# Transposes of the attention weights behind the first row of scores, and layer norm statistics taken one stage earlier

## The chip, the cores and the metric

One core of a Trainium2 chip runs one program. The metric is the device time of that program in microseconds, the median of several runs. The engines are TensorE (PE; its weight loads are listed as PEld), VectorE (DVE), ScalarE (ACT), GpSimd (POOL) and SyncE (SP), which here issues DMAs. Each runs its own list of instructions in order; semaphores connect them.

## The reference

The input x has 1024 tokens of 512 numbers (32 sequences of 32). Six layers follow one another, each added to x and each reading the layer norm of x:

```python
x = x + L0_xattn(layernorm(x), ctx)   # cross-attention, causal
x = x + L0_attn(layernorm(x))         # windowed, gated
x = x + L0_ffn(layernorm(x))          # 64 experts, top 8
x = x + L1_xattn(layernorm(x), ctx)   # cross-attention, 257 context rows, 16 heads of 64
x = x + L1_attn(layernorm(x))         # rotary attention, 16 heads of 32, alibi
x = x + L1_ffn(layernorm(x))          # 8 experts, top 2
# layernorm: (x - mean) / sqrt(var + 1e-5) over the 512 numbers of a token
```

The change touches the fourth and the fifth. In the fourth, each sequence of 32 tokens attends to the 257 rows of its own context: scores, softmax over the 257, weights times context. All is in f32.

## The kernel before

x lies in SBUF throughout, as 8 tiles of 128 tokens (4 sequences each). Each stage has one function per engine (`cross_pe`, `cross_dve`, `cross_act`; `attention_pe`, ...), written out in the order in which the engine is to work; the order is by hand, with no planner. Counters (`Counts`) turn that order into semaphore values.

Fourth layer, `cross_pe`. The key projection is folded into the queries, so that for one sequence the scores are 4 rows of blocks (`rt`, 128 head-and-token rows each) by 257 context rows: `scores(b)` (L567), four matmuls in the program for each row of blocks, two instructions each. DVE takes the maxima of the four (`maxima`, L1091 to L1096), ACT the exponentials (L1321), DVE normalises (`normalise`, L1103, L1107) and signals `s_p`. `turn_weights` (L571) then transposes the weights on PE in three groups of four 128x128 blocks (all by L259): first the last context column, broadcast; then context rows 0 to 127; then 128 to 255. The groups alternate between two PSUM banks (TP), so a group waits until ACT has copied out the group two before it (`act_take`, L1223). `mix(b)` (L588) multiplies context by the turned weights in four steps over two other banks (PROJ), which DVE takes (`take_mix`, L1112). A tile on PE (L620) goes: for sequences 0 to 2, `turn_weights`, `scores(b + 1)`, `mix(b)`; for sequence 3, `turn_weights`, then `pe_turn_xn` (transposes of the next tile's normalised x, L271), then its `mix`; then the next tile's queries (L534, L555), heads (L601), `scores(0)` of the next tile between the two halves of the heads, and the output projection (L615). The last tile (`final`) has no next tile to prepare.

A tile on DVE (L1128) ends with `layernorm` of tile i + 2 (L709: statistics L713, aggregation L715, inverse root L692 to L706 in small steps on one column, normalise step L720), then `add_to_x(i)` (L1124, L1126). For i = 6 the layer norm is that of tile 0 for the fifth layer. After the eight tiles L1170 signals `s_end["xattn1"]`. SP waits for it to load the fifth layer's value weights, output weights (L1446) and the last layer's eight experts (L1577), in that order. Query and key weights are loaded earlier.

Fifth layer, `attention_pe`/`attention_dve` with `rope=True`. PE per tile: queries and keys (L302), `values` (L352), the value projection (L302), transposes of rotated queries and keys (L259), score matmuls of 32x32 (L329), transposes of the next xn (L259), output projection (L365). `scores` waits for ACT's copies of the turned queries and keys and, but for the first tile, for `take_out` (L855). DVE per tile: rotation of queries and keys (L757 to L761), `layernorm(i + 2)`, `take_out`, softmax (L818 to L841) with the additions to x (L801) in between. Ahead of the loop, with no `take_out`, stands `layernorm(dve, 1)`. The first value projection waits for its weights' load.

Of the kernel before, what the change touches and what calls it, by code (L numbers as in the profile page):

```python
# [10 lines left out]
ALU = mybir.AluOpType  # L11
# [4 lines left out]
B, S, D = 32, 32, 512  # L16
TILES = B * S // P
# [14 lines left out]
EPS = 1e-5  # L32
# [33 lines left out]
def wait(eng, sem, value):  # L66

    if not isinstance(value, int) or value > 0:
        eng.wait_ge(sem, value)
# [35 lines left out]
def build(nc, t):  # L105
    with ExitStack() as ctx:
        def sb(name, words, dt=F32):
            return ctx.enter_context(nc.sbuf_tensor(name, [P, words], dt))[:, :]

        def sem(name):  # L110
            return ctx.enter_context(nc.semaphore(name))

        def carve(buf, base, *sizes):

            for n in sizes:
                assert base + n <= buf.shape[1], (base, n)
                yield buf[:, base:base + n]
                base += n


        x = sb("x", TILES * D)
# [20 lines left out]
        xn, xnT = carve(work, 0, D, D)  # L142
# [29 lines left out]
        def some(n, at=[0]):  # L172
            at[0] += n
            assert at[0] <= 1240, at
            return small[:, at[0] - n:at[0]]

        stats, mv, var, half, root, step = some(6), some(2), some(1), some(1), some(1), some(1)
        negmax, total, inv, restp = some(H), some(H), some(H), some(H)
        blockmask, causal, rshare = some(S), some(S), some(TILES)
        keymask = some(TILES * S)  # L180
# [21 lines left out]
        s_xn = sem("xn_ready")  # L202
# [17 lines left out]
        s_ctxT = [sem("ctx_columns_even"), sem("ctx_columns_odd")]  # L220
# [21 lines left out]
        def pe_project(pe, c, emit, banks=2):  # L242

            wait(pe, s_proj_free, c.proj.value(banks - 1))
            emit(bank[PROJ + c.proj.n % banks]).then_inc(s_proj, 1)
            c.proj.add()
# [7 lines left out]
        def pe_transpose(pe, c, pieces):  # L254

            wait(pe, s_tp_free, c.tp.value(1))
            to = bank[TP + c.tp.n % 2]
            for j, src in enumerate(pieces):
                done = nc.tensor.transpose(to[:, j * P:(j + 1) * P], src, ident[:, :])  # L259
            done.then_inc(s_tp, 1)  # L260
            c.tp.add()

        def pe_turn_xn(pe, c, parts, banks=2):
            c.xn.add()
            wait(pe, s_xn, c.xn.value())
            n = KD // parts
            for part in range(parts):
                def emit(to):
                    for j in range(n):
                        at = (part * n + j) * P  # L270
                        done = nc.tensor.transpose(to[:, j * P:(j + 1) * P], xn[:, at:at + P], ident[:, :])  # L271
                    return done
                pe_project(pe, c, emit, banks)
# [250 lines left out]
        def cross_pe(pe, c):  # L524
# [14 lines left out]
            def turn_q():  # L539
                for half_ in range(2):  # L540
                    wait(pe, s_proj_free, c.proj.value(1 - half_))
                    pe_transpose(pe, c, [q1[:, (half_ * 4 + j) * P:(half_ * 4 + j + 1) * P] for j in range(4)])
# [16 lines left out]
                    c.proj.add()  # L559
                    c.tp.add()  # L560

            def scores(b):
                c.ctxT[b % 2].add(16)
                wait(pe, s_ctxT[b % 2], c.ctxT[b % 2].value())
                for rt in range(4):
                    for j in range(KD):
                        done = nc.tensor.matmul(bank[SCORE + rt][:, 0:NCTX], qpv[:, j, b, rt * P:(rt + 1) * P],  # L567
                                                ctxT[b % 2][:, j * NCTX:(j + 1) * NCTX], start=(j == 0), stop=(j == KD - 1))
                    done.then_inc(s_s, 1)

            def turn_weights():  # L571

                c.p.add(4)
                wait(pe, s_p, c.p.value())
                pe_transpose(pe, c, [p1[:, (rt + 1) * NCTX - 1:(rt + 1) * NCTX].broadcast_to([P, P]) for rt in range(4)])
                for kc in range(2):
                    pe_transpose(pe, c, [p1[:, rt * NCTX + kc * P:rt * NCTX + (kc + 1) * P] for rt in range(4)])

            def mix(b, turned):

# [38 lines left out]

            def tile(final):  # L620
                for b in range(SEQS - 1):
                    turn_weights()
                    turned = c.tp.value()
                    scores(b + 1)
                    mix(b, turned)
                turn_weights()
                turned = c.tp.value()
                if not final:
                    pe_turn_xn(pe, c, 1)
                mix(SEQS - 1, turned)  # L630
                mixed = c.proj.value()
                if not final:
                    project_q(KD)
                    turn_q()
                    queries_wk()
                wait(pe, s_proj_free, mixed)
                out_heads(0)
                if not final:
                    wait(pe, s_proj_free, c.proj.value(1))
                    wait(pe, s_tp_free, c.tp.value())  # L640
                    scores(0)
                out_heads(1)
                project_out()
# [46 lines left out]
        def inverse_roots(dve, var, half, root, step):  # L690

            nc.vector.tensor_single_scalar(half.bitcast(I32), var.bitcast(I32), 1, ALU.logical_shift_right)  # L692
            dve.drain()
            nc.vector.tensor_scalar(root.bitcast(I32), half.bitcast(I32), -1.0, float(0x5F3759DF), ALU.mult, ALU.add)
            for _ in range(3):
                dve.drain()
                if var.free_size() == 1:
                    nc.vector.scalar_tensor_tensor(step, root, var, root, ALU.mult, ALU.mult)
                else:
                    nc.vector.tensor_tensor(step, root, var, ALU.mult)  # L700
                    dve.drain()
                    nc.vector.tensor_tensor(step, step, root, ALU.mult)
                dve.drain()
                nc.vector.tensor_scalar(step, step, -0.5, 1.5, ALU.mult, ALU.add)
                dve.drain()
                nc.vector.tensor_tensor(root, root, step, ALU.mult)  # L706
            dve.drain()

        def layernorm(dve, i):  # L709

            xt = x[:, bass.ds(i * D, D)]
            dve.drain()
            nc.vector.bn_stats(stats, xt)  # L713
            dve.drain()
            nc.vector.bn_aggr(mv, stats)  # L715
            dve.drain()
            nc.vector.tensor_scalar(var, mv[:, 1:2], EPS, None, ALU.add)
            dve.drain()
            inverse_roots(dve, var, half, root, step)
            nc.vector.tensor_scalar(xn, xt, mv[:, 0:1], root, ALU.subtract, ALU.mult).then_inc(s_xn, 1)  # L720

        def statistics(dve):

# [22 lines left out]
        def attention_dve(dve, st, c):  # L746
# [120 lines left out]
            def tile(i, ln=True, rest=False, tails=SEQS):  # L867
                seqs = iter(range(tails if st.cross else 0))

                def sums():  # L870
                    for _ in range(tails // 4):
                        for b in seqs:
                            sum_tail(b, i + 1)
                            break
                first(sums)
                if ln:
                    if st.gated and (not isinstance(i, int) or i + 2 < TILES):
                        dve.drain()
                        correct(i + 2)
                    layernorm(dve, i + 2 if not isinstance(i, int) else (i + 2) % TILES)  # L880
                take_out()
                if rest:
                    take_rest()
                if "v" not in st.by_act:
                    take("v")
                if rest:
                    take_turned_rest()

                def between():
                    if rest:  # L890
                        take_rest_out()
                    add_to_x(i, 0)
                softmax(i + 1, between, lambda: add_to_x(i, 1))
# [9 lines left out]
            if st.cross:  # L903
                dve.wait_ge(s_w["bias_vo0"], 16 * 3)
            if st.rope:
                layernorm(dve, 1)
            if "v" not in st.by_act:
                take("v")
            if st.cross:
# [151 lines left out]
        def cross_dve(dve, c):  # L1061
# [60 lines left out]
            def add_to_x(i):  # L1122
                xt = x[:, bass.ds(i * D, D)]
                dve_take(dve, c, lambda src: nc.vector.tensor_tensor(xt, xt, src, ALU.add))  # L1124
                dve.drain()
                nc.vector.tensor_tensor(xt, xt, bo1, ALU.add)  # L1126

            def tile(i, final):  # L1128
                for b in range(SEQS - 1):
# [531 lines left out]
```

## Time and profile before

| | us |
|---|---|
| median of 3 runs | 2520.74 |
| lowest, highest | 2514.85, 2523.68 |
| profiled execution, device time | 2523.09 |
| profiled execution, span of its instructions | 2521.2 |
| fourth layer (second cross-attention) | about 1296 to 2066 |
| fifth layer (rotary attention) | about 2066 to 2240 |

PE is the busiest engine; DVE is busy 44% of the span, ACT 13%. In all rows the start is counted in microseconds from the start of the span, and "idle <-" gives the idle time of the engine just before the instruction and what ended it. The granted clock (PEclk) is 1.00 at 2.4 GHz and 0.50 at 1.2 GHz; a value between is the mean of a stretch that had both.

### The profile page before, as it was taken

The numbers are of one execution on the slowest core, as the hardware profiler recorded it, in microseconds if no ns is written. First come the engines' busy times: TensorE is split into PE (matmuls) and PEld (weight loads), VectorE is DVE, ScalarE is ACT, GpSimd is POOL, SyncE is SP. The second block draws the span as 40 slices with busy tenths as digits, with TensorE's granted clock in tenths as the row PEclk, the third lists the DMA queues.
The fourth block names the chain that finished last, engine by engine and source line by source line (L and its number), as shares of the span: only waits on it lengthen the run. The fifth ranks groups of instructions, "written<-read, shape, count | busy, mean of one in ns | idle before, by whom it ended". The sixth has DMA issues, their size and how long they took to land. (4 is left out here: it accounts for less than half of the span.)

```text
span 2521.2 us, 48836 instructions
## 1 busy us (share of the span) xinstructions
PE 2324.2 (92%) x19338; PEld 1695.1 (67%) x19338; DVE 1116.2 (44%) x3030; ACT 321.9 (13%) x753; POOL 213.5 (8%) x266
## 2 busy tenths in 40 slices
PE   6999899997369999999979999999999999979999
PEld 5887688986258888888856766766766755544444
DVE  3666332333644444444334444444444436634333
ACT  0000011110001111111112222222222211100000
POOL 0000000000014333333310000000000000000000
PEclk8999899999579999999989999999999999989999
DMA  6224500002429999999951111111111132000000
GB/s 251 67 67 167 151 32 0 0 0 77 163 89 333 326 329 336 331 324 333 334 152 59 34 42 58 33 45 55 33 47 53 34 134 96 0 2 9 8 8 8
DMA packets 64677, 291.18 MB, mean 115 GB/s; under 512 B 9079, under 2 KB 9591, under 8 KB 55264
## 3 DMA queue, kind: packets, MB, share of 16 engines
q1 hardware_dynamic: 46976, 247.50, 27.1%
q0 software_dynamic: 16480, 40.62, 6.3%
q10 hardware_dynamic: 1152, 2.10, 0.2%
q8 instruction: 49, 0.80, 0.1%
q14 instruction: 20, 0.16, 0.0%
HBM read 268.45 MB, written 23.13 MB: 116 GB/s over the span
## 5 line engine op out<-in xcount | busy, mean ns | idle before, releaser
L493 PEld LDWEIGHTS psum<-work,arena 128*128 128x128 f32 x3072 | 354.4, 193 | 31.7 <-issue 30.8
L493 PE MATMUL psum<-work,arena 128*128 128x128 f32 x3072 | 355.0, 276 | 1.4 <-ACT work L1282 1.4
L296 PEld LDWEIGHTS psum<-work,arena 128*128 128x128 f32 x2560 | 293.0, 194 | 8.7 <-issue 4.8
L296 PE MATMUL psum<-work,arena 128*128 128x128 f32 x2560 | 293.8, 277 | 3.0 <-ACT work L1223 1.7
L672 PE MATMUL psum<-arena,work 128*128 128x512 f32 x512 | 233.9, 620 | 0.0
L567 PE MATMUL psum<-work,arena 128*128 128x257 f32 x1024 | 229.6, 381 | 0.8 <-DVE arena L1084 0.8
L1223 ACT COPY work<-psum 128x512 f32<-128x512 f32 (+2 forms) x200 | 102.6, 540 | 985.9 <-PE psum L259 835.7
L588 PE MATMUL psum<-work 128*128 128x512 f32 x512 | 225.7, 594 | 2.9 <-ACT work L1223 2.2
L567 PEld LDWEIGHTS psum<-work,arena 128*128 128x128 f32 x1024 | 192.1, 190 | 29.4 <-issue 1.2
L302 PE MATMUL psum<-arena,work 128*128 128x512 f32 x448 | 199.7, 597 | 1.4 <-ACT work L1223 1.4
L672 PEld LDWEIGHTS psum<-arena,work 128*128 128x128 f32 x512 | 101.0, 199 | 126.5 <-issue 126.2
L501 PE MATMUL psum<-arena,work 128*128 128x512 f32 x384 | 182.0, 610 | 2.0 <-DVE work L1035 2.0
L588 PEld LDWEIGHTS psum<-work 128*128 128x128 f32 x512 | 96.5, 190 | 113.3 <-issue 98.5
L365 PE MATMUL psum<-arena,work 128*128 128x256 f32 x640 | 156.0, 405 | 3.7 <-DVE work L855 2.4
L302 PEld LDWEIGHTS psum<-arena,work 128*128 128x128 f32 x448 | 83.1, 190 | 95.8 <-issue 93.7
L365 PEld LDWEIGHTS psum<-arena,work 128*128 128x128 f32 x640 | 129.6, 206 | 23.5 <-DVE work L855 2.6
L1112 DVE SCALAR_TENSOR_TENSOR arena<-work,psum 128x512 f32<-128x512 f32 x128 | 95.5, 746 | 101.5 <-PE psum L588 101.5
L259 PE MATMUL psum<-ident,work 128*128 128x128 f32 x616 | 95.9, 287 | 37.1 <-DVE work L720 20.5
L1091 DVE TENSOR_REDUCE small<-psum 128x1 f32<-128x257 f32 x128 | 54.2, 424 | 171.5 <-PE psum L567 170.5
L259 PEld LDWEIGHTS psum<-ident,work 128*128 128x128 f32 x616 | 72.0, 144 | 77.5 <-issue 40.5
L501 PEld LDWEIGHTS psum<-arena,work 128*128 128x128 f32 x384 | 68.1, 190 | 64.6 <-issue 61.8
L1041 DVE TENSOR_SCALAR work<-psum,small 128x512 f32<-128x512 f32 x64 | 48.0, 751 | 130.4 <-PE psum L501 102.4
(174 smaller groups left out, 2217.6 us busy)
## 6 DMA issues: line engine op xcount, KB each, us to landing
arena<-in_experts SPq DMA_DIRECT2D x64, 2304.0 KB, 10.0
work<-in_ctxT SPq DMA_DIRECT2D x32, 514.0 KB, 4.3
work<-in_ctx SPq DMA_DIRECT2D x32, 512.0 KB, 3.8
work<-in_ctx_tail SPq DMA_DIRECT2D x32, 450.0 KB, 3.4
arena<-in_experts SPq DMA_DIRECT2D x8, 1024.0 KB, 18.3
arena<-in_qkv SPq DMA_DIRECT2D x1, 6144.0 KB, 19.2
arena<-in_o SPq DMA_DIRECT2D x2, 2048.0 KB, 18.7
arena<-in_q SPq DMA_DIRECT2D x1, 2048.0 KB, 8.9
```

Of the source, the lines that this page charges most:

```text
L259: done = nc.tensor.transpose(to[:, j * P:(j + 1) * P], src, ident[:, :])
L296: done = nc.tensor.matmul(to[:, n * P:(n + 1) * P], w[:, j, at:at + P], src[:, j * P:(j + 1) * P], start=(j == 0), stop=(j == KD - 1))
L302: done = nc.tensor.matmul(to, src[:, j * P:(j + 1) * P], w[:, j, half_ * BANK:(half_ + 1) * BANK], start=(j == 0), stop=(j == KD - 1))
L365: done = nc.tensor.matmul(to[:, 0:D // 2], oT[:, j * P:(j + 1) * P], w[:, j, half_ * D // 2:(half_ + 1) * D // 2], start=(j == 0), stop=(j ...
L493: done = nc.tensor.matmul(to[:, n * P:(n + 1) * P], w[:, at:at + P], xgT[e % 2][:, j * P:(j + 1) * P], start=(j == 0), stop=(j == KD - 1))
L501: done = nc.tensor.matmul(bank[5 + e % 2], hid[e % 2][:, j * P:(j + 1) * P], w[:, j * D:(j + 1) * D], start=(j == 0), stop=(j == INTER // ...
L567: done = nc.tensor.matmul(bank[SCORE + rt][:, 0:NCTX], qpv[:, j, b, rt * P:(rt + 1) * P], ctxT[b % 2][:, j * NCTX:(j + 1) * NCTX], start=( ...
L588: done = nc.tensor.matmul(to, ctxr[b % 2][:, at:at + P], pT1[:, kc * 4 * P:(kc + 1) * 4 * P], start=(kc == 0), stop=(kc == 1))
L672: done = nc.tensor.matmul(to[:, 0:n], xnT[:, j * P:(j + 1) * P], w[:, j * n:(j + 1) * n], start=(j == 0), stop=(j == KD - 1))
L1091: nc.vector.tensor_reduce(negmax[:, rt:rt + 1], bank[SCORE + rt][:, 0:NCTX], AX.X, ALU.max, negate=True)
L1112: dve_take(dve, c, lambda src: nc.vector.scalar_tensor_tensor(utv[:, j, :, b, :], plast[b % 2].rearrange("p (h n) -> p h n", h=H), last, s ...
L1223: done = nc.scalar.copy(to, src)
```

## The change

On PE, `turn_weights` gets something to issue between its second and its third group. For sequences 0 to 2 this is the first of the four rows of the next sequence's scores, with the wait for that sequence's columns; the other three rows follow the third group. For sequence 3 it is the transposes of the next tile's normalised x; in the last tile it is nothing.

On DVE, `add_to_x(i)` of the fourth layer is followed by `measure(i)`: statistics and inverse root of tile i, kept in two columns of `small`. In the fifth layer, `layernorm` of tiles 1 to 7 becomes `layernorm_measured`, which is the normalise step alone. `layernorm` of tile 0, at both ends of the fifth layer, stays whole.

```diff
+        mean1, root1 = some(TILES), some(TILES)
...
-            def scores(b):
-                c.ctxT[b % 2].add(16)
-                wait(pe, s_ctxT[b % 2], c.ctxT[b % 2].value())
-                for rt in range(4):
+            def scores(b, rows=range(4)):
+                if rows[0] == 0:
+                    c.ctxT[b % 2].add(16)
+                    wait(pe, s_ctxT[b % 2], c.ctxT[b % 2].value())
+                for rt in rows:
...
-            def turn_weights():
+            def turn_weights(meanwhile):
...
                 for kc in range(2):
                     pe_transpose(pe, c, [p1[:, rt * NCTX + kc * P:rt * NCTX + (kc + 1) * P] for rt in range(4)])
+                    if kc == 0:
+                        meanwhile()
...
                 for b in range(SEQS - 1):
-                    turn_weights()
+                    turn_weights(lambda: scores(b + 1, range(0, 1)))
                     turned = c.tp.value()
-                    scores(b + 1)
+                    scores(b + 1, range(1, 4))
                     mix(b, turned)
-                turn_weights()
+                turn_weights(lambda: None if final else pe_turn_xn(pe, c, 1))
                 turned = c.tp.value()
-                if not final:
-                    pe_turn_xn(pe, c, 1)
                 mix(SEQS - 1, turned)
...
+        def measure(dve, i):
+
+            dve.drain()
+            nc.vector.bn_stats(stats, x[:, bass.ds(i * D, D)])
+            dve.drain()
+            nc.vector.bn_aggr(mv, stats)
+            dve.drain()
+            nc.vector.tensor_copy(mean1[:, bass.ds(i, 1)], mv[:, 0:1])
+            nc.vector.tensor_scalar(var, mv[:, 1:2], EPS, None, ALU.add)
+            dve.drain()
+            inverse_roots(dve, var, half, root, step)
+            nc.vector.tensor_copy(root1[:, bass.ds(i, 1)], root)
+
+        def layernorm_measured(dve, i):
+            dve.drain()
+            nc.vector.tensor_scalar(xn, x[:, bass.ds(i * D, D)], mean1[:, bass.ds(i, 1)], root1[:, bass.ds(i, 1)],
+                                    ALU.subtract, ALU.mult).then_inc(s_xn, 1)
+
...
-                    layernorm(dve, i + 2 if not isinstance(i, int) else (i + 2) % TILES)
+                    if st.rope and (not isinstance(i, int) or i + 2 < TILES):
+                        layernorm_measured(dve, i + 2)
+                    else:
+                        layernorm(dve, i + 2 if not isinstance(i, int) else (i + 2) % TILES)
...
             if st.rope:
-                layernorm(dve, 1)
+                layernorm_measured(dve, 1)
...
                 nc.vector.tensor_tensor(xt, xt, bo1, ALU.add)
+                measure(dve, i)
```

## Rows read from the trace of the kernel before

**Rows 1.** The page: busy time, share of the span, instructions of TensorE

```profile
PE 2324.2 (92%) x19338; PEld 1695.1 (67%) x19338; DVE 1116.2 (44%) x3030; ACT 321.9 (13%) x753; POOL 213.5 (8%) x266
```

**Rows 2.** Windows, the steady part of the cross-attention: length, busy per engine, PEclk, DMA, GB/s

```profile
1444.00:2065.00 621.00, 609.01 (x3530) 412.86 (x3529) 277.95 (x686) 130.28 (x349) 0.00 (x0) 1.00 0.14 49
```

**Rows 3.** Waits of TensorE, 1430 to 2066: total us, times, longest

```profile
PE psum L259 <- ACT work L1223: 6.5, 27, 0.2
```

**Rows 4.** Time order, TensorE, cross-attention: start us, us, engine, line, operands [idle <-releaser]

```profile
1726.05 1.04 PE L259 MATMUL psum<-ident,work 128*128 128x128 f32 x8
1727.32 0.66 PE L259 MATMUL psum<-ident,work 128*128 128x128 f32 x4 [0.24 <-ACT work L1223]
1727.81 7.12 PE L567 MATMUL psum<-work,arena 128*128 128x257 f32 x32
...
1758.51 0.66 PE L259 MATMUL psum<-ident,work 128*128 128x128 f32 x4 [0.24 <-ACT work L1223]
1759.00 0.60 PE L271 MATMUL psum<-ident,work 128*128 128x128 f32 x4
1759.91 7.13 PE L588 MATMUL psum<-work 128*128 128x512 f32 x16 [0.31 <-ACT work L1223]
```

**Rows 5.** Time order, TensorE, last tile of the cross-attention

```profile
2041.29 0.66 PE L259 MATMUL psum<-ident,work 128*128 128x128 f32 x4 [0.24 <-ACT work L1223]
2042.66 7.10 PE L588 MATMUL psum<-work 128*128 128x512 f32 x16 [0.72 <-issue]
```

**Rows 6.** Time order, VectorE, end of one tile of the cross-attention and next scores

```profile
1705.84 0.69 DVE L713 BATCH_NORM_STATS2 small<-x 128x6 f32 x1 [0.25 <-issue]
...
1709.86 0.55 DVE L720 TENSOR_SCALAR work<-x,small 128x512 f32 x1
...
1711.54 0.69 DVE L1126 TENSOR_TENSOR x<-x,arena 128x512 f32 x1
...
1719.38 0.42 DVE L1091 TENSOR_REDUCE small<-psum 128x1 f32<-128x257 f32 x1 [1.31 <-PE psum L567]
```

**Rows 7.** Time order, all engines, from the cross-attention to the rotary attention

```profile
2066.00 10.57 PE L302 MATMUL psum<-arena,work 128*128 128x512 f32 x24 [0.68 <-ACT work L1223]
2066.47 0.15 DVE L1170 COPY small<-small 128x1 f32<-128x1 f32 x1
2066.65 0.38 SPq L1446 DMA_DIRECT2D arena<-in_av  x1
```

**Rows 8.** DMA issues of 2066 to 2080: KB each, median us to landing

```profile
arena<-in_av SPq DMA_DIRECT2D x1, 1024.0 KB, 5.4
```

**Rows 9.** Time order, TensorE and VectorE, first two tiles of the rotary attention

```profile
2077.24 0.66 PE L259 MATMUL psum<-ident,work 128*128 128x128 f32 x4 [0.24 <-ACT work L1223]
...
2078.66 0.54 PE L329 MATMUL psum<-work 32*32 32x32 f32 x41 [0.77 <-ACT work L1223]
...
2094.03 0.66 PE L259 MATMUL psum<-ident,work 128*128 128x128 f32 x4 [0.24 <-ACT work L1223]
...
2095.33 0.68 DVE L855 COPY work<-psum 128x512 f32<-128x512 f32 x1
2096.11 1.08 PE L329 MATMUL psum<-work 32*32 32x32 f32 x105 [1.43 <-DVE work L855]
```

**Rows 10.** Windows, tiles of the rotary attention, columns as in rows 2

```profile
2076.40:2096.11 19.71, 16.25 (x301) 8.89 (x300) 15.07 (x44) 4.54 (x8) 0.00 (x0) 1.00 0.93 385
2096.11:2117.54 21.43, 19.76 (x309) 12.38 (x310) 13.21 (x33) 2.88 (x5) 0.00 (x0) 0.92 0.00 2
2117.54:2137.32 19.78, 18.13 (x309) 11.10 (x309) 13.32 (x33) 2.88 (x5) 0.00 (x0) 1.00 0.00 0
2137.32:2158.62 21.30, 19.65 (x309) 12.29 (x309) 13.22 (x33) 2.88 (x5) 0.00 (x0) 0.92 0.00 0
...
2178.40:2199.56 21.16, 19.61 (x308) 12.31 (x309) 13.22 (x33) 2.88 (x5) 0.00 (x0) 0.92 0.00 0
...
2219.24:2240.00 20.76, 13.74 (x284) 11.04 (x285) 6.16 (x11) 0.63 (x1) 0.00 (x0) 0.69 0.01 2
```


## The prediction

> **What bounds the kernel now.** I read the page first: TensorE (PE) is busy 92% of the span [rows 1]. Then the stage windows: through the second cross-attention PE works 609 of 621 us at a full granted clock [rows 2]. So there only what stands between two PE instructions counts, and the list of PE's own waits names it: it stops 27 times, 0.24 us each, for a ScalarE (ACT) copy at the transposes [rows 3]. In time order, each sequence issues eight transposes, stops, issues four more, then goes straight on with the scores; the tile's last sequence stops once more, 0.31 us ahead of its mix [rows 4]. The stop is the third group waiting for the bank of the first. VectorE (DVE) has room here, so its work costs nothing unless a wait of PE ends on it. The rotary attention behind it is different. There PE stops 1.43 us per tile, and what ends the stop is DVE's L855 copy, which stands directly behind a layer norm [rows 9]. So the order on PE decides in one stage, the order on DVE in the next.
>
> **Part 1, third group behind the first row of scores.** Eight transposes at the pace of the third group (four in 1727.81 - 1727.32 = 0.49) are issued in 0.98 us, and the third group starts 1.27 after the first: 0.29 us is lost per sequence [rows 4]. With one quarter of the scores (7.12/4 = 1.78 us) between, the bank has been copied out long before. The gain is full for sequences 0 to 2 of each tile: 24 x 0.29 = -7.0 us. What is late next is the mix, which needs the copy of the third group; that now ends 1.5 us later, but three quarters of the scores (5.3 us) cover it. The extra changes from matmul to transpose and back have no row in this exact place. Their nearest rows say zero (third group to scores starts 0.49 later, its plain pace [rows 4]); I take zero, and bound it by half the present stop, 0.12 each, 2.9 us in all. A gain is excluded, as nothing is removed with them. The wait for the columns of the next sequence moves ahead of the third group, and behind it on PE are now those four transposes and the mix. The scores directly behind it were waiting for the same load before, and never stopped [rows 3].
>
> For the last sequence of seven tiles the four transposes of the normalised tile come between instead. Before, from the end of the eighth issue to the mix: 0.29 stop + 1.40 (1758.51 to 1759.91), where 0.49 of that 1.40 is the normalised tile's transposes, lying under the copy [rows 4]. After: these 0.49 first, then the third group with nothing under its copy. The last tile shows that case: 1.37 from the group to the mix [rows 5]. So 0.49 + 1.37 - 1.69 = +0.17, times 7 = +1.2 us. The wait that is removed comes back as a longer wait for the copy. The last tile keeps its order: 0.
>
> **Part 2, statistics measured in this stage.** From the statistics' start to the normalise step a layer norm takes 1709.86 - 1705.84 = 4.02 us [rows 6]. The new step is this plus two copies of one column, each near the 0.15 us of the L1170 copy [rows 7], so 4.3 us. In seven tiles it runs beside PE's scores. DVE is free at 1712.2, would be busy until 1716.6, then has three row maxima of 0.42 to do before the fourth row arrives at 1719.4 [rows 6]: over 1 us is left, less 0.3 by part 1. Cost 0. Were this cover gone, what is behind it on DVE (maxima, then ACT's exponentials) would stop PE seven times.
>
> In the eighth tile nothing covers it. The signal of the stage's end (L1170) stands behind the new step, and the loads of the value and output weights wait for this signal on SyncE (SP), the eight expert loads behind them [rows 7]. The value weights' load was issued at 2066.65 and took 5.4 us, so landed at 2072.05 [rows 7, 8]. PE's 24 projection matmuls take 10.57 us from 2066.00 on, and the last eight, the value projection, start at 2073.05 [rows 7]: a reserve of 1.0 us. The load comes 4.3 later, so PE stops 3.3 us, with everything else queued behind it: +3.3. No other issue of SP matters; the experts' transfers are first read a stage later. Bounds: +2.3 (a load 1 us quicker) to +5.
>
> In rotary attention the layer norm shrinks to its last step in six tiles; the one that restores tile 0 for the experts stays whole. DVE then reaches L855 some 3.9 us sooner. But the scores also wait for ACT's copy of the turned keys. The first rotary tile, where there is no L855, shows it: 2078.66 - 2077.24 = 1.42 from the second transposes to the scores, with a stop of 0.77 ended by ACT; in the loop 2096.11 - 2094.03 = 2.08 [rows 9]. The gain is only the difference, 0.66, in five tiles, and about 0.5 in the sixth, where the stop is shorter because the index is fixed and DVE computes no address: -3.8 us. DVE is not missed elsewhere.
>
> **The clock.** Tiles of the rotary stage alternate between a granted clock of 0.92 and of 1.00: three of the six up to 2219 are long (21.43, 21.30, 21.16), the three between and behind them short, like the one of 19.78 [rows 10]. A long tile thus spent part of its time at the 1.2 GHz level, and it costs 1.65, 1.52 and 1.38 against 19.78. PE's sparse part in each is the transposes, the stop, and the small score matmuls. The first rotary tile, with the stop of 0.77 that I forecast, ran through at a clock of 1.00 [rows 10]. So I expect the three falls to go: -4.6 us, with bounds 0 and -4.6. On the other side the new stop of 3.3 us ahead of the value projection is longer than any here, and the stretch from 2219 on, with the sparse end of the stage, was granted 0.69 [rows 10]. I price that at one more fall, +1.6, bounds 0 and 3.
>
> The Trainium skill, "TensorE: Matmul & The Clock Gate", section "HAM oscillation — how this bites in real kernels", tells of a kernel whose clock fell at every wait for a DMA between bursts of matmuls. This speaks against the change at the stage boundary; no row shows such a stop yet. By it the +1.6 stands, without it the sum would be 1.6 lower.
>
> **Sum.** -7.0 + 1.2 + 3.3 - 3.8 - 4.6 + 1.6 = -9.3 us. The profiled execution took 2523.09 (span 2521.2, 1.9 around it), which gives 2513.8. It was 2.35 over the median of the three runs, within their spread of 8.8, so I subtract from the median: 2520.7 - 9.3 = **2511.4 us**.
>
> **Rivals.**
> (a) The clock falls go on. For it: the transposes and the 32-wide score matmuls stay, only 0.66 us of stop goes. Against: the first rotary tile. It costs back the 4.6: 2516.0. The same page, section "Part 4: PE-mode transpose", says that transposes do not count as work for the clock in the way of matmuls. By that rule the cause would be left in place and this rival would hold; the first rotary tile, with the same transposes at clock 1.00, speaks against it.
> (b) The boundary is dearer: the load lands in 9 instead of 5.4 us beside other transfers. For it: the output weights' load, issued 0.4 us behind it, took longer. Against: it is still the first in the queue. 2515.
> (c) The boundary is cheap: no stop worth the name, or full clock. Against: the reserve of only 1.0 us. 2511.4 - 4.9 = 2506.5.
> (d) The second part does not bring what it says: the scores wait for something else as long as before, no 3.8 and no 4.6. Against: the copy's 1.42 in rows 9. 2519.8.
> (e) Slower: breaking the run of matmuls costs PE itself, at each of the 24 places where transposes now stand between two rows of scores, because weights are no longer loaded ahead. It decides from (9.3 + 7.6)/24 = 0.7 us each; at 0.8 the time is 2511.4 + 24 x 0.8 = 2530.6. Against: the present change from transposes to scores costs nothing in [rows 4].
>
> **Chances.** Forecast 0.52, (a) 0.16, (b) 0.08, (c) 0.12, (d) 0.07, (e) 0.05. The forecast's own range is 2507 to 2516, from its bounds and half the spread of the runs before. The range 2505 to 2518.5 takes in (a), (b) and (c) and leaves out the lowest end of (c), (d) and (e). 0.3% is 7.6 us, about what a measurement of this kernel tells from no change, so faster means below 2513.1. The forecast is there with some 0.7 (0.36), (c) nearly always (0.11), (a) and (b) together 0.05: 0.52. Slower is (e) alone, 0.05; the rest, 0.43, is within 0.3%.
>
> **What would show it.** In the cross-attention: no idle time ahead of the third group except in the last tile, a period of a sequence shorter by 0.29, but a mix stop of about 0.9 in place of 0.31 after the normalised tile. At the boundary: the value projection starts about 4.3 us after the same point of the load, with an idle PE of 3.3. In the rotary tiles: the scores 1.42 behind the transposes, released by ACT, and all six periods near 19.1 at clock 1.00. I am wrong if maxima on DVE begin to hold PE in the cross-attention, if the load lands as early as before, or if periods of 20.6 stay in the rotary stage.

## The result, and the profile after

The changed kernel takes 2514.29 us in the median of 18 runs, the kernel before 2524.68 in 18 runs beside it. The ratio of the two is 0.9957 with a 95% interval of 0.9941 to 0.9973, so the change is worth 0.43%, some 10.9 us (6.8 to 14.9). The profiled execution took 2515.07 (span 2513.1).

TensorE has as much to do as before and is as busy as in [rows 1]:

```profile
PE 2318.5 (92%) x19338; PEld 1693.8 (67%) x19338; DVE 1120.7 (45%) x3060; ACT 321.8 (13%) x753; POOL 214.3 (9%) x266
```

The stage windows say where the time went. Columns: stretch, its length, busy time and count of PE, PEld, DVE, ACT, POOL, then PEclk, DMA share, GB/s. First the kernel before: the cross-attention from its first query projection to the first rotary projection, the rotary projections up to the next transposes, and the six repeated rotary tiles:

```profile
1300.30:2066.00 765.70, 745.85 (x4321) 507.18 (x4321) 346.74 (x863) 162.72 (x433) 0.00 (x0) 0.99 0.15 52
2066.00:2076.40 10.40, 10.40 (x24) 4.61 (x25) 5.52 (x12) 0.00 (x0) 0.00 (x0) 1.00 0.78 280
...
2093.20:2216.43 123.23, 113.40 (x1849) 70.29 (x1848) 79.66 (x199) 17.25 (x30) 0.00 (x0) 0.96 0.01 4
```

The same three stretches after:

```profile
1306.20:2061.42 755.22, 739.48 (x4320) 506.67 (x4320) 367.76 (x975) 162.67 (x433) 0.00 (x0) 0.99 0.16 53
2061.42:2076.95 15.53, 12.37 (x25) 5.13 (x26) 8.33 (x27) 0.00 (x0) 0.00 (x0) 0.89 0.59 216
...
2093.64:2208.45 114.81, 108.78 (x1850) 66.63 (x1849) 62.99 (x120) 17.26 (x30) 0.00 (x0) 1.00 0.00 2
```

| stretch | before | after | difference |
|---|---|---|---|
| cross-attention | 765.70 | 755.22 | -10.5 |
| first rotary projections | 10.40 | 15.53 | +5.1 |
| first rotary tile | 16.80 | 16.69 | -0.1 |
| six rotary tiles | 123.23 | 114.81 | -8.4 |
| from there to the last output projection | 18.43 | 18.72 | +0.3 |
| the rest | 286.34 | 285.93 | -0.4 |
| sum | | | -14.0 |

The cross-attention began 5.9 us later in this profile (1306.2 against 1300.3), in stages that the change doesn't touch. The two spans therefore differ by 8.1 only. Up to 716 us the two profiles are within 0.2, so the difference arises in the expert layer. A second profile of each kernel gave 1305.5 and 1300.8, and the kernels of the experiments started the stage anywhere from 1301.8 to 1310.6. Whether the later start belongs to the changed kernel or is chance is not shown. The sum of the stages lies in the interval of the timed runs, near its far end.

One sequence of the cross-attention in time order on PE, answering [rows 4]. The transposes are now L260, the scores L569, the mix L592 (in the next fence):

```profile
1726.46 1.04 PE L260 MATMUL psum<-ident,work 128*128 128x128 f32 x8
1727.33 1.91 PE L569 MATMUL psum<-work,arena 128*128 128x257 f32 x8
1729.08 0.60 PE L260 MATMUL psum<-ident,work 128*128 128x128 f32 x4
1729.51 5.39 PE L569 MATMUL psum<-work,arena 128*128 128x257 f32 x24
...
1741.60 1.04 PE L260 MATMUL psum<-ident,work 128*128 128x128 f32 x8
```

The kernel before reached the same place, from 1726.05 on, at:

```profile
1741.64 1.04 PE L259 MATMUL psum<-ident,work 128*128 128x128 f32 x8
```

There is no idle time left around the third group. From the first transposes to the end of their issue it is 0.87 us for eight, then 1.75 for a row of scores, then 0.43 for the third group. Before, the twelve transposes took 1.76 from the first start to the scores; now 0.87 + 0.43 = 1.30. The period of a sequence is 15.14 (1741.60 - 1726.46) where it was 15.59 (1741.64 - 1726.05).

The last sequence of a tile, with the transposes of the normalised tile (L272) in between, and the stop for the copy ahead of the mix:

```profile
1756.74 1.04 PE L260 MATMUL psum<-ident,work 128*128 128x128 f32 x8
1757.61 0.60 PE L272 MATMUL psum<-ident,work 128*128 128x128 f32 x4
1758.05 0.62 PE L260 MATMUL psum<-ident,work 128*128 128x128 f32 x4
1759.42 2.84 PE L592 MATMUL psum<-work 128*128 128x512 f32 x6 [0.75 <-ACT work L1247]
```

VectorE at the end of a tile, answering [rows 6]: the statistics (L727 to L735) run from 1713.18 to 1717.56, the first three maxima are done together, and the fourth still waits 0.78 us for its row. The cover holds, with that much left:

```profile
1713.18 0.69 DVE L727 BATCH_NORM_STATS2 small<-x 128x6 f32 x1
...
1717.41 0.15 DVE L735 COPY small<-small 128x1 f32 x1 [0.17 <-issue]
1717.93 1.09 DVE L1114 TENSOR_REDUCE small<-psum 128x1 f32<-128x257 f32 x3 [0.36 <-issue]
1719.80 0.42 DVE L1114 TENSOR_REDUCE small<-psum 128x1 f32<-128x257 f32 x1 [0.78 <-PE psum L569]
```

The stage boundary, answering [rows 7, 8]: the 16 matmul instructions of queries and keys, the end signal (L1194) now 4.75 us after the first of them (0.47 before), the load's issue on SP, and the value projection behind a stop of 3.15 us that the load ends. The load took 5.3 us:

```profile
2061.42 7.13 PE L303 MATMUL psum<-arena,work 128*128 128x512 f32 x16 [0.68 <-ACT work L1247]
...
2066.17 0.15 DVE L1194 COPY small<-small 128x1 f32<-128x1 f32 x1
...
2066.35 0.38 SPq L1470 DMA_DIRECT2D arena<-in_av  x1
...
2071.71 4.54 PE L303 MATMUL psum<-arena,work 128*128 128x512 f32 x6 [3.15 <-DMA arena<-in_av]
```

```profile
arena<-in_av SPq DMA_DIRECT2D x1, 1024.0 KB, 5.3
```

The clock fell behind the stop. It was 1.00 through the stop and until 2072.25, half a microsecond after the value projection had begun; from 2072.96 to 2075.50 it was 0.50. From the projection's start to the transposes it is 5.24 us, where eight of the 24 projection instructions at full clock took some 3.5 (10.40/3), and the whole window was granted 0.67:

```profile
2071.71:2076.95 5.24, 5.24 (x9) 2.17 (x10) 0.00 (x0) 0.00 (x0) 0.00 (x0) 0.67 1.03 402
```

A rotary tile, answering [rows 9] and [rows 10]: the scores (L330) come 1.43 us after the second transposes and are released by ACT, not by VectorE, and the tiles take 19.1 us at a clock of 1.00:

```profile
2094.48 0.66 PE L260 MATMUL psum<-ident,work 128*128 128x128 f32 x4 [0.24 <-ACT work L1247]
2095.91 1.28 PE L330 MATMUL psum<-work 32*32 32x32 f32 x128 [0.77 <-ACT work L1247]
```

```profile
2112.78:2131.91 19.13, 18.12 (x310) 11.10 (x309) 10.38 (x19) 2.88 (x5) 0.00 (x0) 1.00 0.00 0
```

### The profile page after: what moved, and what is told of

Its sections match the earlier page's. It is cut to its first block and busy times, and to the rows that moved or that the text cites. A ratio compares the mean times of both kernels' runs of the same rounds, so it can differ in the third digit from the quotient of the medians.

```text
span 2513.1 us, 48907 instructions
## 1 busy us (share of the span) xinstructions
PE 2318.5 (92%) x19338; PEld 1693.8 (67%) x19338; DVE 1120.7 (45%) x3060; ACT 321.8 (13%) x753; POOL 214.3 (9%) x266
## 5 line engine op out<-in xcount | busy, mean ns | idle before, releaser
L569 PE MATMUL psum<-work,arena 128*128 128x257 f32 x1024 | 234.0, 382 | 0.8 <-DVE arena L1107 0.8
L592 PE MATMUL psum<-work 128*128 128x512 f32 x512 | 225.7, 594 | 6.0 <-ACT work L1247 5.3
L569 PEld LDWEIGHTS psum<-work,arena 128*128 128x128 f32 x1024 | 190.7, 191 | 28.1 <-issue 1.2
L592 PEld LDWEIGHTS psum<-work 128*128 128x128 f32 x512 | 96.5, 190 | 116.3 <-issue 94.7
L366 PE MATMUL psum<-arena,work 128*128 128x256 f32 x640 | 150.8, 395 | 3.7 <-DVE work L875 2.3
L1135 DVE SCALAR_TENSOR_TENSOR arena<-work,psum 128x512 f32<-128x512 f32 x128 | 95.6, 747 | 107.6 <-PE psum L592 107.6
L260 PE MATMUL psum<-ident,work 128*128 128x128 f32 x616 | 92.7, 281 | 30.1 <-DVE work L722 20.7
L260 PEld LDWEIGHTS psum<-ident,work 128*128 128x128 f32 x616 | 72.7, 142 | 65.7 <-issue 40.6
L1449 POOL DMA_INDIRECT x_rows<-work,small x64 | 104.8, 1638 | 27.5 <-issue 21.1
## 6 DMA issues: line engine op xcount, KB each, us to landing
arena<-in_o SPq DMA_DIRECT2D x2, 2048.0 KB, 18.5
```

The source lines that it names most:

```text
L366: done = nc.tensor.matmul(to[:, 0:D // 2], oT[:, j * P:(j + 1) * P], w[:, j, half_ * D // 2:(half_ + 1) * D // 2], start=(j == 0), stop=(j ...
L592: done = nc.tensor.matmul(to, ctxr[b % 2][:, at:at + P], pT1[:, kc * 4 * P:(kc + 1) * 4 * P], start=(kc == 0), stop=(kc == 1))
L1135: dve_take(dve, c, lambda src: nc.vector.scalar_tensor_tensor(utv[:, j, :, b, :], plast[b % 2].rearrange("p (h n) -> p h n", h=H), last, s ...
L1449: pool.indirect_dma_start(x_d, bass.IndirectOffsetOnAxis(ap=sidx.bitcast(U32)[:, e % ROUND:e % ROUND + 1], axis=0), y[e % 2], None, bounds ...
```

## The experiments

Each ratio is to the kernel before, run beside the kernel in question. Beside the first four (order, statistics, earlier signal, filled stop) its median was 2524.98, beside the next four 2522.02, and beside the last three, of one run each, 2522.24.

### Each part alone

The order alone, with all layer norms as before:

```diff
             def add_to_x(i):
...
                 nc.vector.tensor_tensor(xt, xt, bo1, ALU.add)
-                measure(dve, i)
...
-                    if st.rope and (not isinstance(i, int) or i + 2 < TILES):
-                        layernorm_measured(dve, i + 2)
-                    else:
-                        layernorm(dve, i + 2 if not isinstance(i, int) else (i + 2) % TILES)
+                    layernorm(dve, i + 2 if not isinstance(i, int) else (i + 2) % TILES)
...
-                layernorm_measured(dve, 1)
+                layernorm(dve, 1)
```

> The changed kernel with the layer norms as before: only the order of the transposes on TensorE is new. Theory (each sequence 0 to 2 saves 0.45 us, the 0.29 of stop that was forecast and 0.16 because groups that never stopped are issued 0.44 and not 0.49 apart; the last sequence saves nothing): the cross-attention, from its first query projection to the first rotary projection, is 24 x 0.45 = 10.8 us shorter than in the kernel before, the rotary stage is as before, three tiles near 21.3 us at a granted clock of 0.92 and three near 19.8 at 1.00, and the median is about 10.8 us below that of before. Rival (only the 0.29 per stop belongs to the order and the rest came with the statistics): the stage is 7 us shorter.

Measured: 2514.1 us, ratio 0.9956 (0.9936 to 0.9977), 11 us less. Windows of the cross-attention and of the first three of the six rotary tiles:

```profile
1301.80:2056.13 754.33, 738.57 (x4320) 506.02 (x4321) 346.87 (x863) 162.70 (x433) 0.00 (x0) 0.99 0.16 53
2083.34:2104.86 21.52, 19.85 (x309) 12.39 (x308) 13.22 (x34) 2.88 (x5) 0.00 (x0) 0.92 0.06 23
2104.86:2125.95 21.09, 19.42 (x310) 12.18 (x309) 13.24 (x34) 2.88 (x5) 0.00 (x0) 0.92 0.00 0
2125.95:2145.74 19.79, 18.12 (x309) 11.11 (x308) 13.32 (x34) 2.88 (x5) 0.00 (x0) 1.00 0.00 0
```

The cross-attention takes 754.33 us, as short as with both parts. So the whole gain of that stage is the order's and the rival falls. Long and short rotary tiles are both still there, four long ones among the six in this profile. In the timed runs the order alone is as good as the whole change (0.9956 against 0.9957, 2514.1 against 2514.29 us). What the statistics add to it is 3.3 us by the stage windows (below), and no timed comparison of these two kernels shows it.

The statistics alone, with the transposes in the old order:

```diff
-                    turn_weights(lambda: scores(b + 1, range(0, 1)))
+                    turn_weights(lambda: None)
                     turned = c.tp.value()
-                    scores(b + 1, range(1, 4))
+                    scores(b + 1)
                     mix(b, turned)
-                turn_weights(lambda: None if final else pe_turn_xn(pe, c, 1))
+                turn_weights(lambda: None)
                 turned = c.tp.value()
+                if not final:
+                    pe_turn_xn(pe, c, 1)
```

> The changed kernel with the order of the transposes as before: only the statistics are taken in the cross-attention. Theory: the cross-attention keeps its length, so the seven covered statistics cost 0; the value projection of the rotary stage stops 3.2 us for its load and its clock falls once (+5.1 us up to the next transposes); six rotary tiles take 19.1 us each at clock 1.00 (-8.4 us). Together about -3 us against before. Rival (the statistics cost something beside the scores, hidden in the changed kernel by the gain of the order): the cross-attention is longer by 1 us or more.

Measured: 2518.27 us, ratio 0.9979 (0.9962 to 0.9995), 5.3 us less with an interval from 1 to 10. Windows of the cross-attention, of the projections at the boundary, and of the six rotary tiles:

```profile
1304.50:2069.15 764.65, 744.79 (x4321) 506.57 (x4321) 367.78 (x975) 162.47 (x433) 0.00 (x0) 1.00 0.15 52
2069.15:2084.69 15.54, 12.36 (x24) 5.12 (x25) 8.32 (x27) 0.00 (x0) 0.00 (x0) 0.89 0.58 212
2101.39:2216.21 114.82, 108.78 (x1850) 66.64 (x1849) 62.98 (x120) 17.25 (x30) 0.00 (x0) 1.00 0.01 2
```

764.65 us is no longer than the kernel before (765.70, and 766.42 in a second profile of it). The seven covered statistics cost nothing. The boundary costs 15.54 - 10.40 = 5.1, the six tiles give back 123.23 - 114.82 = 8.4: 3.3 in all, within the timed interval.

### The signal ahead of the last statistics

```diff
-            def add_to_x(i):
+            def add_to_x(i, final):
...
                 nc.vector.tensor_tensor(xt, xt, bo1, ALU.add)
+                if final:
+                    dve.drain()
+                    nc.vector.tensor_copy(step, step).then_inc(s_end["xattn1"], 1)
                 measure(dve, i)
```

(the signal behind the last tile is taken out)

> The changed kernel, but in the last tile of the cross-attention VectorE signals the end of the stage before it takes the statistics, not after. Theory (the statistics ahead of the signal are what delays the load of the value weights): the load is issued 4.3 us earlier, the value projection does not stop, the clock stays at 1.00 there, and the stage up to the next transposes takes 10.4 us as in the kernel before, not 15.5: about 5 us below the changed kernel, near 16 below before. Rival (the load is late because the memory or the queue is busy at that moment): it lands later than 5.4 us after its issue and most of the stop stays.

Measured: 2504.75 us, ratio 0.9907 (0.9881 to 0.9933). VectorE's signal, SP's issue, and the window from the first rotary projection to the transposes:

```profile
2065.32 0.15 DVE L1152 COPY small<-small 128x1 f32<-128x1 f32 x1
2065.50 0.38 SPq L1471 DMA_DIRECT2D arena<-in_av  x1
```

```profile
2064.84:2075.25 10.41, 10.40 (x25) 4.62 (x25) 8.33 (x27) 0.00 (x0) 0.00 (x0) 1.00 0.80 283
```

10.41 us at a clock of 1.00: stop and fall are gone, and the cause is shown. But by the medians, which were not measured side by side, the kernel is 9.5 us below the changed one and not 5. Its profile differs from that of the changed kernel in more places. From the last repeated tile to the last output projection it takes 12.0 us and not 18.7, which has another cause (see below: TensorE's stops without a releaser). Its cross-attention begins 4.4 us later (1310.6), which takes some of this back. This kernel was profiled a second time, beside the next ones:

> The kernel with the signal ahead of the last statistics once more, on the chip of the others of this call, as the base for the one with the moved transposes: value projection without a stop, tiles of 19.1 us.

It took 2504.84 us, with 10.40 at the boundary and 12.0 at the end again.

### TensorE filled during the stop, in the kernel before

```diff
             def scores(turned):
+                if st.rope:
+                    w = weights[st, "v"].rearrange("p (k n) -> p k n", k=KD)
+                    for j in range(3):
+                        nc.tensor.matmul(bank[PROJ][:, 0:D // 2], xnT[:, j * P:(j + 1) * P], w[:, j, 0:D // 2], start=True, stop=True)
                 wait(*turned)
```

> The kernel before, with three products of 128x256 on TensorE (six instructions, into a bank that is free there and whose result nobody reads) ahead of the wait of the rotary scores. They take some 1.4 us, which lies within the 2.1 us from the second transposes to the scores, so the order and the wait for VectorE stay. Theory (the clock falls because TensorE is idle in that stop): no fall in the six tiles, all take 19.7 to 19.8 us at a granted clock of 1.00, some 4.6 us less than before. Rival (the transposes and the 32-wide products keep the clock down whatever is in the stop): three of the six tiles stay near 21.3 us at 0.92.

Measured: 2518.5 us, ratio 0.9972 (0.9951 to 0.9992). The added products (L324) and the scores behind them, then windows of two of the six tiles (the other four took 19.79 to 19.81 at 1.00):

```profile
2097.68 1.46 PE L324 MATMUL psum<-arena,work 128*128 128x256 f32 x6
2099.28 1.28 PE L333 MATMUL psum<-work 32*32 32x32 f32 x128
```

```profile
2096.35:2116.15 19.80, 19.42 (x315) 12.13 (x314) 13.23 (x34) 2.87 (x5) 0.00 (x0) 1.00 0.05 19
...
2195.35:2215.04 19.69, 19.43 (x315) 12.14 (x314) 13.32 (x33) 2.88 (x5) 0.00 (x0) 1.00 0.01 2
```

Transposes, score matmuls and layer norm are those of the kernel before, and so is the time from the second transposes to the scores (2099.28 - 2097.19 = 2.09). Only PE no longer idles in it. All six tiles are short, at full clock, where the three profiles with the empty stop had three or four falls among six. So in these tiles the transposes and the small products do not bring the fall by themselves. It takes the idle time beside them, and filling that is enough to avoid it. That rules rival (a) of the prediction out, as do the six tiles at 1.00 in each of the two profiles of the changed kernel. Whether transposes count for less than matmuls, as the Trainium skill has it in "TensorE: Matmul & The Clock Gate", section "Part 4: PE-mode transpose", no run here shows.

### The statistics taken twice

```diff
                 measure(dve, i)
+                if not final:
+                    measure(dve, i)
```

> The changed kernel, but each of the seven covered statistics is taken twice (the last tile's once), so VectorE works some 8.5 us between the addition to x and the maxima of the next scores. Theory (there is cover of some 1 us before the last row of maxima is late, and another 2.4 us before TensorE is: the normalised weights are needed only after the mix): TensorE waits 0.3 to 1.5 us per tile at the transposes of the next weights, 2 to 10 us in all. Rival (the cover ends with the last row of maxima): TensorE waits about 3.5 us per tile, 24 us in all.

Measured: 2524.26 us in one run. The cross-attention took 770.14 us, 14.9 more than in the changed kernel, 2.1 per tile. Neither number expected came out. What PE waited for from 1440 to 2070 (us in total, times, longest), and one such place in time order:

```profile
PE psum L592 <- DVE arena L1135: 12.5, 7, 2.1
```

```profile
1730.62 1.42 DVE L1114 TENSOR_REDUCE small<-psum 128x1 f32<-128x257 f32 x4 [0.36 <-issue]
...
1732.62 1.41 DVE L1135 SCALAR_TENSOR_TENSOR arena<-work,psum 128x512 f32<-128x512 f32 x2
...
1733.42 1.55 PE L592 MATMUL psum<-work 128*128 128x512 f32 x3 [1.81 <-DVE arena L1135]
```

The maxima came late, at 1730.62, and behind them on VectorE stood the takes of the mix (L1135). The mix has two banks. PE filled both and stopped in the middle of the mix, 1.8 us, long before the next weights were due. So the cover ends neither with the last maximum nor with the next weights but with the third step of the mix. My list of what stands behind the statistics on VectorE had lacked this.

### All four rows of scores ahead of the third group

```diff
-                    turn_weights(lambda: scores(b + 1, range(0, 1)))
+                    turn_weights(lambda: scores(b + 1))
                     turned = c.tp.value()
-                    scores(b + 1, range(1, 4))
```

> The changed kernel, but for sequences 0 to 2 all four rows of scores stand ahead of the third group of transposes. Theory (the third group needs something behind it to cover its copy, as in the last sequence): no stop ahead of the third group, but one of 0.75 us ahead of each of these mixes, 0.9 us from issue to issue: 24 x 0.9 = 22 us more than the changed kernel, and 11 more than before. Rival (the mix waits for the context rows or the banks anyway): no change.

Measured: 2529.64 us in one run. The waits of PE for the copy ahead of the mix from 1430 to 2070, and the window of the whole stage:

```profile
PE psum L592 <- ACT work L1246: 18.0, 24, 0.8
```

```profile
1305.50:2083.99 778.49, 744.81 (x4320) 506.79 (x4320) 367.24 (x975) 160.38 (x433) 0.00 (x0) 1.00 0.15 51
```

23.3 us more than the changed kernel in the stage (22 expected), 12.8 more than before. The place matters more than the removal of the stop. One row in front and three behind hides both copies. Four in front bare the second.

### The next transposes ahead of the scores

Beside the earlier signal, for the rotary attention only (in its first tile, ahead of the loop, in the same way):

```diff
+                if turn and st.rope:
+                    turn_xn()
                 scores(turned)
                 if rest:
                     rest_out()
-                if turn:
+                if turn and not st.rope:
                     turn_xn()
                 project_out()
```

> The changed kernel with the signal of the stage's end ahead of the last statistics, and in the rotary attention the transposes of the next normalised tile moved ahead of the scores, into the stop in which TensorE waits for the copy of the turned keys. Possible only because the normalise step is early now. Theory: the four transposes (0.44 to 0.49 us) lie in the stop of 0.77, the tiles take 18.6 to 18.7 us instead of 19.1, 3.4 us less over seven tiles than with the signal alone, some 8.5 us below the changed kernel. Rival (they need the bank whose copy the scores wait for, or ScalarE does them first): the stop moves behind them and nothing is gained.

Measured: 2502.6 us, ratio 0.9914 (0.9892 to 0.9937). A tile in time order and its window:

```profile
2103.36 0.60 PE L260 MATMUL psum<-ident,work 128*128 128x128 f32 x4
2104.20 1.14 PE L260 MATMUL psum<-ident,work 128*128 128x128 f32 x8 [0.24 <-ACT work L1253]
2105.62 1.28 PE L330 MATMUL psum<-work 32*32 32x32 f32 x128 [0.28 <-ACT work L1253]
```

```profile
2103.36:2122.10 18.74, 18.22 (x309) 11.13 (x308) 10.29 (x19) 2.78 (x5) 0.00 (x0) 1.00 0.00 0
```

The eight transposes are now issued as one group behind the stop, and the scores wait 0.28 instead of 0.77. Tiles take 18.74 us. The first one is shorter by 1.3, since the next projections no longer wait for their copy. From the first rotary projection to the last tile's transposes it is 138.24 us against 141.92 with the signal alone, 3.7 less. Expected were 3.4, but otherwise divided: six tiles give 0.4 each, and the 1.3 of the first was not foreseen. In the timed runs this does not show: 2502.6 against 2504.75, not measured side by side, with intervals that overlap. This kernel had the stops of the next paragraph in both its profiles, the one with the signal alone in none.

### Stops that nobody releases

> The changed kernel once more. Open: in its first profile TensorE stops twice, 2.41 and 2.84 us, for nothing but its own instructions in the last tile of the rotary attention, each time while a 16 KB instruction transfer starts, and its clock falls behind them; from the last transposes to the last output projection it takes 18.7 us. In the kernel with the signal ahead of the last statistics, whose list for TensorE is the same, it took 12.0 us in both looks. Theory (the stops come with the layout of each program and stay with a kernel): 18.7 us again. Rival (they come and go from run to run of the same kernel): 12 to 13 us in some of these looks.

> The kernel with the moved transposes once more. Its first profile has the two stops too, 17.6 us from the last transposes to the last output projection. Theory (they stay with a kernel): 17.6 again and some 2502 in all. Rival (they vary from run to run): about 12 us there, and 2497 in all.

> The kernel before once more. Theory (the stops stay with a kernel): 18.4 us from the last transposes of the rotary stage to the last output projection, as in its first profile. Rival (they vary): 12 to 13 us. In either case the rotary tiles of 21.3 and 19.8 us are there again, three or four long ones among six.

In the last tile of the rotary stage PE stops twice inside its small matmuls, with nothing but "issue" as the reason, here in the changed kernel:

```profile
2214.84 0.35 PE L330 MATMUL psum<-work 32*32 32x32 f32 x14 [2.41 <-issue]
...
2225.83 0.41 PE L353 MATMUL psum<-work 32*32 32x32 f32 x31 [2.84 <-issue]
```

A 16 KB transfer of the instruction queue begins within 0.6 us of the start of each such stop. The stretch has such transfers where PE does not stop too, so that they cause the stops is not shown. The second profiles, of single runs of 2513.79, 2504.59 and 2518.05 us, gave 18.5 us for this stretch in the changed kernel (18.7 in the first), 17.9 in the one with the moved transposes (17.6), and in the kernel before 12.0, where its first profile had 18.4. Windows of the kernel before, first and second profile:

```profile
2216.43:2234.86 18.43, 9.87 (x281) 7.70 (x279) 7.95 (x18) 2.29 (x4) 0.00 (x0) 0.78 0.01 3
```

```profile
2218.82:2230.82 12.00, 7.47 (x282) 6.13 (x280) 7.96 (x18) 2.29 (x4) 0.00 (x0) 1.00 0.01 3
```

So the kernel before has both forms, and the theory that they stay with a kernel falls. For the changed kernel two profiles of two had the long one, for the kernel with the earlier signal none of two, and that is too few to say more. Of all 13 profiles six have the two stops: one of the kernel before, both of the changed one, the one of the order alone, and both with the moved transposes. The second profile of the kernel before also had 21.1 to 21.5 us in four of its six rotary tiles, 19.8 in two.

## Why the prediction was right, and where it was not

Predicted were 2511.4 us and -9.3, that is 0.37%; measured 0.43% and 2514.29, in the range. The median of before moved up by 3.9 us with more runs. From that median the forecast would have been 2515.4, 1.1 above what was measured. That the sum came so near is in part luck. The stage windows give -14.0 and not -9.3: the order brought 4.7 us more than its term. In the span of the profile the start 5.9 us later took more than that back.

1. **The order, -7.0 + 1.2 = -5.8.** Measured -10.5 between the two profiles and 24 x 0.45 = -10.8 from the periods. This is the mis-sized term. The mechanism and the place were right, but I took the issue time of the third group as the plain pace, 0.49 for four. That group had just stopped. Groups that don't stop take 0.43 to 0.44 for four and 0.87 for eight. So a stop cost 0.45 and not 0.29. The +1.2 of the last sequence came to zero for the same reason: 2.68 us from the first transposes to the mix before and after (1759.42 - 1756.74). The copy was indeed left bare, with a stop of 0.75 in place of 0.31, where about 0.9 was forecast. The 0.45 that the third group gave back paid for it, and for the transposes that now lie bare.
2. **Changes between matmul and transpose, 0.** Right: third group to scores 0.43, scores to third group at the scores' pace. Rival (e) is out.
3. **Statistics under the scores, 0.** Right: shown by the statistics alone, with 0.78 us left where I had "over 1, less 0.3". What I named as the price of a lost cover was incomplete, as the doubled statistics showed.
4. **The boundary, +3.3 and +1.6.** Measured a stop of 3.15 and 5.1 in all. Its cause is shown by the kernel with the earlier signal, where both are gone. Rival (c) is out, and so is (b): the load took 5.3 us. The Trainium skill's account of a clock that falls at a wait for a DMA, in "TensorE: Matmul & The Clock Gate", section "HAM oscillation — how this bites in real kernels", agrees with the trace here: 0.67 in the window behind the stop, after 1.00 in the stop itself. In the kernel with doubled statistics the value projection itself kept its clock and the next projections lost it (8.75 us for 7.13); the price was the same.
5. **The rotary tiles, -3.8 and -4.6.** Measured -8.4 together. 1.43 us from transposes to scores, 19.13 per tile, no fall. Rival (d) is out. That the falls hung on the idle time in the stop is shown by the filled stop, in the kernel before and with its wait unchanged.
6. The steps by profile add up to -14.0 and the timed difference is -10.9 with an interval that holds both. The stops without a releaser, worth 6 us in one stretch, are in one of the two profiles of the kernel before and in both of the changed one. The start of the cross-attention was 5.9 us later in the first pair of profiles and 4.8 in the second. How much either adds to the difference of the medians stays open. So does the rest of the 9.5 us of the kernel with the earlier signal.

## What to carry to other kernels

Take a group's plain pace from a place where it did not wait. A group behind a stop is slower itself, and removing the stop is worth more than the idle time that the profile shows. When work is moved off one stage, look at what the last round of the other stage does with it. There it stood ahead of an end signal and a load, and cost more than half of what it gave (5.1 of 8.4 us), and the timed runs don't tell the whole change from the order alone. Put behind the signal it cost nothing, and that kernel was faster than both (ratio 0.9907 to the kernel before).

## What the runs showed of the hardware that I had not expected

In one execution of the kernel before TensorE stopped 2.07 and 2.83 us in the last rotary tile with no releaser that the profile shows, in another of the same kernel not at all. With the clock falls behind them the stretch took 18.4 or 12.0 us. Matmuls whose result nobody reads, put into a stop of TensorE, made the kernel faster: six tiles of 19.8 us instead of three or four long ones of 21.1 to 21.5, at the same wait. The clock falls of these tiles had a pattern, never none and never all: three of six in one profile of the kernel before, four in the other, and four in that of the order alone.
